# Weighted layer of a graph network: adjacency blocks in a ring of two, built between the products

## What is computed

```python
msgs = feat[src_idx] * affine[:, None]
agg = jax.ops.segment_sum(msgs, dst_idx, num_segments=feat.shape[0])
gcn_feat = jnp.concatenate([feat, agg], axis=-1)
out = gcn_feat @ mlp_w.T + mlp_b
```

## Time and profile before

| | us |
|---|---|
| median of 3 runs | 3364.9 (3363.34 to 3366.77) |
| the profiled execution's own time | 3366.92 |
| its span in the trace | 3365.2 |
| its mean granted TensorE clock | 0.922 of full speed |
| the list of steps of the third layer, first build to first product behind it | 1530.6 to 2197.0 |
| busy over the span: TensorE, GpSimd, VectorE, ScalarE | 2892.9, 2182.4, 1785.0, 1142.1 |

### The profile page before, as it was taken

The page is one execution under the profiler, slowest core; times in us unless marked ns, Lnnn a source line. Parts: engine busy times, 40 slices in busy tenths (PEclk is TensorE's granted clock), DMA queues, the critical chain, the costliest instruction groups (busy, mean ns, idle before and its releaser), DMA issues. The chain is left out here.

```text
span 3365.2 us, 61823 instructions
## 1 busy us (share of the span) xinstructions
PE 2892.9 (86%) x22719; PEld 2463.9 (73%) x22719; DVE 1785.0 (53%) x5589; ACT 1142.1 (34%) x1908; POOL 2182.4 (65%) x2179
## 2 busy tenths in 40 slices
PE   1699999999799989987999999967988887877885
PEld 0477777778688868866778777766988787777775
DVE  6899996233423334347766757556433333333334
ACT  2655554000200001014656656543522222222223
POOL 3465552777477666747777777317777777777772
PEclk9799999999899999998999999968988888888886
DMA  7355555888677777862222222123222222222222
GB/s 161 137 179 191 189 190 187 285 278 279 213 247 270 268 253 241 285 212 43 44 47 46 46 47 46 24 54 82 54 52 46 53 46 52 53 45 53 53 45 50
DMA packets 163977, 433.17 MB, mean 129 GB/s; under 512 B 63604, under 2 KB 105514, under 8 KB 143581
## 3 DMA queue, kind: packets, MB, share of 16 engines
q1 hardware_dynamic: 93998, 304.72, 25.6%
q0 software_dynamic: 69680, 124.50, 16.7%
HBM read 335.49 MB, written 93.53 MB: 127 GB/s over the span
## 5 line engine op out<-in xcount | busy, mean ns | idle before, releaser
L829 POOL DMA_INDIRECT work_all<-parts_dram,idx_all x768 | 809.6, 1054 | 357.6 <-issue 228.0
L1414 PE MATMUL ps<-arena 128*128 128x288 bf16 x7154 | 1023.5, 288 | 0.0
L2002 POOL DMA_INDIRECT arena<-table,idx_all x696 | 663.6, 953 | 325.0 <-issue 210.3
L1414 PEld LDWEIGHTS ps<-arena 128*128 128x128 bf16 x7154 | 711.8, 100 | 174.1
L2304 PE MATMUL ps<-M,arena 128*128 128x96 f32 x1664 | 424.9, 355 | 172.3 <-DVE arena L2187 169.3
L1561 POOL DMA_INDIRECT arena<-table,idx_all x400 | 405.6, 1014 | 121.9 <-issue 121.3
L2304 PEld LDWEIGHTS ps<-M,arena 128*128 128x128 f32 x1664 | 324.0, 242 | 192.4 <-issue 190.9
L1245 PE MATMUL ps<-arena,spare 128*128 128x245 bf16 x975 | 291.8, 305 | 30.5 <-ACT arena L882 18.5
L2306 PE MATMUL ps<-arena 128*128 128x96 bf16 x2496 | 291.2, 235 | 0.0
L1805 PE MATMUL ps<-work_all,gathot 128*128 128x245 f32 x1100 | 277.2, 390 | 14.1 <-DVE gathot L1655 12.0
L882 ACT ACTIVATE arena<-ps 128x980 bf16<-128x980 f32 x234 | 231.2, 990 | 166.5 <-PE ps L1245 166.5
(11 more groups left out here) (407 smaller groups left out, 4553.3 us busy)
## 6 DMA issues: line engine op xcount, KB each, us to landing
arena<-blocks_dram SPq DMA_DIRECT2D x117, 1568.0 KB
blocks_dram<-arena SPq DMA_DIRECT2D x39, 1568.0 KB, 6.5
arena<-table,idx_all POOLq DMA_INDIRECT x1096
parts_dram<-arena SPq DMA_DIRECT2D x28, 504.0 KB, 3.2
work_all<-parts_dram,idx_all POOLq DMA_INDIRECT x768
arena<-eaT_dram SPq DMA_DIRECT2D x10, 624.0 KB, 5.2
eaT_dram<-arena SPq DMA_DIRECT2D x48, 104.0 KB, 2.5
arena<-qtable SPq DMA_DIRECT2D x104, 45.0 KB
```

Of the source, the lines that this page charges most:

```text
L829: eng.indirect_dma_start(out=gat_rows[kk % 3][:, u, :], out_offset=None, in_=parts_dram[:, :], in_offset=bass.IndirectOffsetOnAxis(ap=idx_ ...
L1414: last = nc.tensor.matmul(apply_ps[n % 2], blk[m % 3][:, b, :], Hs[:, b, :], start=b == 0, stop=b == NB - 1)
L2002: eng.indirect_dma_start(out=rows[g % NROW][:, u, :], out_offset=None, in_=table[:, :], in_offset=bass.IndirectOffsetOnAxis(ap=idx_all[:, ...
```

## The change

`wadj` becomes a ring of two blocks of 125 targets, in the same room. The list of steps is written anew: TensorE builds block 0 and four tiles more (29 tiles), then in each block 49 products of 125 columns, with 21 tiles of the next block built between them, one after every second or third product, and behind the last product four tiles of the block after that (LEAD). There are 22 rounds of 49 products in place of 11. The copies to `wadj` are 13 a block, the last of one tile; three PSUM banks take builds and one, always the same, takes the products. The first product of a block waits for all copies of that block and for the addition of the block before. Groups, edge features and node units are spread over the list by a clock in which a build counts 2 and a product 1.

```diff
@@ -53,10 +53,10 @@
     WBLK, WFIRST = 22, 44
-    PAIRS, PB, PT = WBLK // 2, 2 * BW, 2 * VW
+    PB, WUNITS = 2 * BW, -(-VW // 2)
     NODEW, NTW, NWG = WBLK * BW, WBLK * VW, NG - WFIRST
     NVW = -(-NTW // NVT)
...
@@ -1483,34 +1483,60 @@
         ws_rel, ws_w, ok_col = small[:, 40:41], small[:, 48:49], small[:, 56:57]
         sum_ps = ps6[0:F, 0:P]
         er_banks = ps45
-        build_ps = [flat(t[:, 4 * i:4 * i + 4, :])[:, 0:2 * KW].rearrange("p (b d) -> p b d", d=2 * WN) for t in (ps01, ps23) for i in range(2)]
+        build_ps = [flat(t[:, 4 * i:4 * i + 4, :])[:, 0:2 * KW].rearrange("p (b d) -> p b d", d=2 * WN) for t, i in ((ps01, 0), (ps01, 1), (ps23, 0))]
         def dense_ps(m):
-            bank = ((m + 1) * (PT // 2) + 3) % 4
-            return flat((ps01, ps23)[bank // 2][0:F, bank % 2 * 4:bank % 2 * 4 + 4, :])[:, 0:PB]
-        STEPS = PT + NB
-        TOTAL = PAIRS * STEPS
-        GROUP_AT = {(2 * k + 1) * TOTAL // (2 * NWG): k for k in range(NWG)}
-        EDGE_AT = {(2 * e + 1) * TOTAL // (2 * NG): e for e in range(NG)}
-        SUM_AT = {s + 4: k for s, k in GROUP_AT.items()}
-        ADD_AT = {(m + 1) * STEPS: m for m in range(PAIRS - 1)}
-        NODE_AT = {8 + (TOTAL - 40) * i // NODE_UNITS: i for i in range(NODE_UNITS)}
-        NODE_LAG = 4
+            return flat(ps23[0:F, 4:8, :])[:, 0:BW]
+        def ring(m):
+            return m % 2 * BW
+        def unit_tiles(u):
+            m, j = divmod(u, WUNITS)
+            return range(m * VW + 2 * j, m * VW + min(2 * j + 2, VW))
+        LEAD = 4
+        STEPS = []
+        for m in range(-1, WBLK):
+            ready = LEAD + m * VW + VW if m >= 0 else 0
+            inside = [] if m < 0 else [ready + (b + 1) * (VW - LEAD) // NB for b in range(NB)]
+            done = ready
+            for b, upto in enumerate(inside):
+                STEPS.append((False, m, b))
+                STEPS += [(True, t, 0) for t in range(done, min(upto, NTW))]
+                done = upto
+            STEPS += [(True, t, 0) for t in range(done, min(LEAD + (m + 2) * VW, NTW))]
+        TOTAL = len(STEPS)
+        assert sum(is_build for is_build, _, _ in STEPS) == NTW and TOTAL == NTW + WBLK * NB
+        CLOCK = [0]
+        for is_build, _, _ in STEPS:
+            CLOCK.append(CLOCK[-1] + (2 if is_build else 1))
+        def spread(count, first, last):
+            at = [first + (last - first) * (2 * i + 1) / (2 * count) for i in range(count)]
+            return {next(s for s in range(TOTAL) if CLOCK[s + 1] > a): i for i, a in enumerate(at)}
+        BUILD_AT = {t: s for s, (is_build, t, _) in enumerate(STEPS) if is_build}
+        LAST_AT = {m: s for s, (is_build, m, b) in enumerate(STEPS) if not is_build and b == NB - 1}
+        EVAC_AT = {BUILD_AT[unit_tiles(u)[-1]]: u for u in range(WBLK * WUNITS)}
+        assert all(BUILD_AT[unit_tiles(u)[0]] > LAST_AT[u // WUNITS - 2] for u in range(2 * WUNITS, WBLK * WUNITS))
+        GROUP_AT = spread(NWG, 0, CLOCK[-1])
+        EDGE_AT = spread(NG, 0, CLOCK[-1])
+        SUM_AT = {s + 9: k for s, k in GROUP_AT.items()}
+        ADD_AT = {LAST_AT[m]: m for m in range(WBLK - 1)}
+        NODE_AT = spread(NODE_UNITS, 16, CLOCK[-1] - 64)
+        NODE_LAG = 8
...
-        def built_at(s):
-            m, j = divmod(s, STEPS)
-            return m * PT + j if j < PT else None
+        assert len(GROUP_AT) == NWG and len(EDGE_AT) == NG and TOTAL // NWG > 10
...
@@ -1595,12 +1621,13 @@
                         eng.wait_ge(nd_mm, ND0 + i - 1)
                     nc.scalar.activation(node_xT[i % 2][0:F, 0:wide], node_T_ps[:, 0:wide], ACT.Copy).then_inc(nd_xT, 1)
-                def evacuate(q):
-                    eng.wait_ge(built, BUILT0 + 2 * q + 2)
-                    m, j = divmod(q, PT // 2)
-                    if m and j == 0:
-                        eng.wait_ge(wapplied, m)
-                    nc.scalar.activation(wadj[:, :, 2 * j * WN:2 * (j + 1) * WN], build_ps[q % 4], ACT.Copy).then_inc(evac, 1)
+                def evacuate(u):
+                    tiles, m = unit_tiles(u), u // WUNITS
+                    eng.wait_ge(built, BUILT0 + tiles[-1] + 1)
+                    if m >= 2 and u % WUNITS == 0:
+                        eng.wait_ge(wapplied, m - 1)
+                    at, wide = ring(m) + tiles[0] % VW * WN, len(tiles) * WN
+                    nc.scalar.activation(wadj[:, :, at:at + wide], build_ps[u % 3][:, :, 0:wide], ACT.Copy).then_inc(evac, 1)
...
@@ -1614,9 +1641,8 @@
                     nc.scalar.activation(er_sq[0:F, :], er_out[0:F, :], ACT.Square, accum_out=erst[e % 2][:, 1:2]).then_inc(er_stat, 1)
                 for s in range(TOTAL):
-                    t = built_at(s)
-                    if t is not None and t % 2:
-                        evacuate(t // 2)
+                    if s in EVAC_AT:
+                        evacuate(EVAC_AT[s])
                     if s in NODE_AT:
                         turned_rows(NODE_AT[s])
                     if s in EDGE_AT:
@@ -1701,7 +1727,7 @@
                     eng.wait_ge(wapplied, m + 1)
                     if groups:
                         eng.wait_ge(acc_done, groups)
-                    nc.vector.tensor_tensor(aggT[:, m * PB:(m + 1) * PB], aggT[:, m * PB:(m + 1) * PB], dense_ps(m), ALU.add).then_inc(added, 1)
+                    nc.vector.tensor_tensor(aggT[:, m * BW:(m + 1) * BW], aggT[:, m * BW:(m + 1) * BW], dense_ps(m), ALU.add).then_inc(added, 1)
...
@@ -1715,28 +1741,29 @@
                 link.done()
                 stray_sums()
                 hots(0)
-                groups = 0
+                groups = dense = 0
                 for s in range(TOTAL):
-                    t = built_at(s)
+                    is_build, t, _ = STEPS[s]
                     if s in ADD_AT:
                         add_dense(ADD_AT[s], groups)
-                    if t is not None and t + WKEYS - 1 < NTW:
+                        dense += 1
+                    if is_build and t + WKEYS - 1 < NTW:
                         keys(t + WKEYS - 1)
                     if s - 2 * NODE_LAG in NODE_AT:
                         node_sums(NODE_AT[s - 2 * NODE_LAG])
                     if s in SUM_AT:
-                        into_nodes(SUM_AT[s], s // STEPS)
+                        into_nodes(SUM_AT[s], dense)
                         groups += 1
                     if s in GROUP_AT and GROUP_AT[s] + 1 < NWG:
                         hots(GROUP_AT[s] + 1)
                     if s in EDGE_AT and EDGE_AT[s]:
                         add_stats(EDGE_AT[s] - 1)
                 for k in range(groups, NWG):
...
@@ -1797,18 +1824,19 @@
                 def build_tile(t):
                     eng.wait_ge(keys_up, BUILT0 + t + 1)
-                    q = t // 2
-                    if t % 2 == 0 and q >= 4:
-                        eng.wait_ge(evac, EVAC0 + q - 3)
-                    if t % PT == 6 and t > PT:
-                        eng.wait_ge(added, t // PT)
-                    nc.tensor.matmul(build_ps[q % 4][:, :, (t % 2) * WN:(t % 2 + 1) * WN], wsrchot[t % WKEYS],
+                    m, j = divmod(t, VW)
+                    u = m * WUNITS + j // 2
+                    if j % 2 == 0 and u >= 3:
+                        eng.wait_ge(evac, EVAC0 + u - 2)
+                    nc.tensor.matmul(build_ps[u % 3][:, :, (j % 2) * WN:(j % 2 + 1) * WN], wsrchot[t % WKEYS],
                                      wkeyhot[t % WKEYS][:, 0:KW].rearrange("p (b d) -> p b d", d=WN), start=True, stop=True).then_inc(built, 1)
                 def apply(m, b):
                     if b == 0:
-                        eng.wait_ge(evac, EVAC0 + (m + 1) * PT // 2)
-                    last = nc.tensor.matmul(dense_ps(m), X[:, b, :], wadj[:, b, :], start=b == 0, stop=b == NB - 1)
+                        eng.wait_ge(evac, EVAC0 + (m + 1) * WUNITS)
+                        if m:
+                            eng.wait_ge(added, m)
+                    last = nc.tensor.matmul(dense_ps(m), X[:, b, :], wadj[:, b, ring(m):ring(m) + BW], start=b == 0, stop=b == NB - 1)
...
@@ -1835,11 +1863,11 @@
                 eng.wait_ge(k_link, 12)
                 stray_products()
                 for s in range(TOTAL):
-                    t = built_at(s)
-                    if t is not None:
-                        build_tile(t)
+                    is_build, i, b = STEPS[s]
+                    if is_build:
+                        build_tile(i)
                     else:
-                        apply(s // STEPS, s % STEPS - PT)
+                        apply(i, b)
...
```

More of the change, by code:

```diff
@@ L55, in build @@
     WBLK, WFIRST = 22, 44
-    PAIRS, PB, PT = WBLK // 2, 2 * BW, 2 * VW
+    PB, WUNITS = 2 * BW, -(-VW // 2)
     NODEW, NTW, NWG = WBLK * BW, WBLK * VW, NG - WFIRST
     NVW = -(-NTW // NVT)
-    assert WBLK % 2 == 0 and PB * 4 <= 1024 and 4 * NVT <= 512 and NVW == 5 and NODEW <= NODE0 and WFIRST <= GFIRST
```

(14 more changed lines are left out.)

## The result

The changed kernel takes 3318.7 us (median of 4 runs, 3317.7 to 3319.9) beside 3365.8 for the kernel before on the same chip: a ratio of 0.9858, interval 0.9841 to 0.9874, **47 us faster**. The forecast was 3323 with a range of 3308 to 3348 and a chance of 0.90 for faster.

A forecast was written before the change was run, and what follows sets the result against it. VectorE was taken to bound the building stretches, GpSimd to be a close second floor. List end 2153.8 against 2197.0 gave gain 43, taken as 42: 3366.9 to 3324.9, less 2.0 for the median, 3323 us; range 3308 to 3348.

The forecast's parts named there:

- the 59 us: Building stretches of the kernel before: 359.5 us, 59 more than TensorE needs, laid to VectorE's pace of making keys.
- VectorE's work hardly changes, 72%: Whole list: VectorE's 445.5 us of work stays, spread over some 620 us, so 72% busy.
- Products of 125 columns, 0.107 a record: Applying blocks: 2156 narrow product records at 0.107 us each, 230.7 us in place of 228.5.
- Start, 1.8 + 3: List start: 1.8 us lost to the half-rate clock, 3 us to the first 29 tiles going at VectorE's pace.
- Block starts, 7: Twenty-one block starts: first products wait for the last copy, 7 us in all, between 0 and 52.
- What I had costed at nothing: Between products: VectorE's additions, keys, 286 copies and three build banks were said to add no waits, 0 us.
- GpSimd sets the end: 2153.8 against TensorE's 2145.7: List end: GpSimd's last gathers hold it at 2153.8 us; TensorE alone would be there at 2145.7.
- my own formula: List end by GpSimd: last gather's end 2144.0, landing 2.5, group 59's products 1.3, last steps 5.0, addition and start 1.0.
- The announced waits for gathered rows: Near the list's end: TensorE's groups would stand waiting for gathered rows, taking what TensorE gained beyond GpSimd's 2153.8 us.
- Load-bound products: Rival, narrow products: weight loads set 0.165 us a record, list 740 us, 3439 us in all; chance 0.05.
- ScalarE taking over at the block starts: Rival, block starts: 1.7 us each, 36 instead of 7, gain 22, 3343 us; chance 0.18 shared with slower GpSimd.
- GpSimd slower when builds go on all the time: Rival, gathers: cadence 1.36 us, list end 2178, gain 19, 3346 us; chance 0.18 shared with late ScalarE.

The follow-up runs named there:

- run 2: Kernel before, key compare left out for all tiles behind the first seven: ratio 0.991, list of steps 634.8 us.
- run 3: Kernel before, each tile's key compare split into two of half the width: ratio 1.0118, building stretches 405.6 us where they took 359.5.
- run 4: Changed kernel, each tile's key compare split into two of half the width: ratio 0.9852 to the kernel before, list 622.5 us.
- run 6: Changed kernel with LEAD = 0, no tiles of the next block before a block's first product: ratio 0.9914 to the kernel before, list 643.2 us.
- run 5: Changed kernel with LEAD = 25, ring of two blocks kept but nothing built between products: 3340.4 us, ratio 0.9915 to the kernel before, list 644.7 us.
- run 9: Changed kernel, two of eight gathers left out in each group behind the first six: median 3318.0 us, ratio 0.9852 to the kernel before.
- run 7: Changed kernel, four of eight edge-feature products left out in 103 of 104 groups: 3316.1 us, ratio 0.9845 to the kernel before.
- run 1: Kernel before, each pair applied as two passes of 125-column products, nothing built between them: ratio 1.0002, list 666.2 us.
- the second profile: Changed kernel unedited, run and profiled once more: 3318.0 us, ratio 0.9852 to the kernel before, list 622.4 us.

## Why the prediction was right, point by point

- **VectorE was what the building half waited for.** Shown in both directions (runs 2 and 3), and that the change frees TensorE from it (run 4). But the 59 us have two causes, and the prediction laid nearly all of them to the first: run 2 leaves some 28 us standing while the waits for keys have nearly gone, and most of these stand for the last copy of each pair. The change covers this wait with the lead tiles (run 6) and the one for keys with the spreading (run 5). The sum priced the block starts by themselves, at 7 us, so it did not suffer.
- **VectorE's work hardly changes, 72%.** It reads 471.8 us, 76%, where 445.5 stood. The durations of its instructions, summed by line, rose only from 555.7 to 559.4 us, 1.7 of it for the additions. The rest of the 26 is overlap that is gone: busy time counts overlapping instructions once, and spread out they overlap by 88 us instead of 110.
- **Products of 125 columns, 0.107 a record.** Measured 0.106 in the change and 0.1075 by itself. The choice of row (same stationary form, cadence and not duration) was the one that mattered for the sign.
- **Start, 1.8 + 3.** The 29 tiles took 19.5 us with 58 build records, two groups and three edge groups, 16.1 us of work: 3.4 lost where 4.8 was priced, granted clock 0.90.
- **Block starts, 7.** 4.6 us on the load row, 2.5 of them the last start alone (2.1 on the product row), the one with a single tile before it:

```profile
2135.49 0.58 PE L1831 MATMUL ps<-work_all,gathot 128*128 128x245 f32 x2
2138.17 4.09 PE L1839 MATMUL ps<-arena,X 128*96 128x125 f32 x36 [2.10 <-ACT arena L1630]
```

  ScalarE's edge groups delayed few of the others. What I had costed at nothing, keys and copies in front of builds, took 4.4 (6.4 less the 2.0 among the first 29 tiles) and 2.1.
- **GpSimd sets the end: 2153.8 against TensorE's 2145.7.** This is the step that failed. The end came at 2151.7 and TensorE set it, 6 us later than its own sum said: 1.1 because the list began at 1531.7, the rest mainly the waits before builds just named and build records at 0.210 between products, where the sum has 0.207. GpSimd's last gather,

```profile
2136.28 0.95 POOL L1587 DMA_INDIRECT work_all<-table,idx_all  x1 [0.30 <-issue]
```

  ended at 2137.2, 6.8 us earlier than before. That is a cadence of (2137.2 - 1515.9) / 480 = 1.294 in place of 1.31, and rows landed after 1.7 us, not 2.5. With these two values my own formula gives 2137.2 + 1.7 + 1.3 + 5.0 + 1.0 = 2146.2, 5.5 us ahead of TensorE's end. The announced waits for gathered rows did not come in either profile, fewer gathers gained nothing (run 9), and the waits appeared only when TensorE was relieved by 22.7 us (run 7) or, for 1.9 us, when the gathers went slower (run 5). The two errors, 8 us too late for GpSimd and 6 too early for TensorE, met near the truth. That the forecast end is within 2.1 us of the measured one is luck; that it lies in the range is not, since the floor of either engine does.
- **The rivals.** Load-bound products: no (run 1). ScalarE taking over at the block starts: no, though without the lead tiles it would have been 23 us (run 6). GpSimd slower when builds go on all the time: it went slightly faster.
- **The size.** 42 us forecast; 47 in the medians, 46.5 in the list, 44.0 with the second profile. The sum had no term for the clock behind the start: some 3.5 us lost before the change, 0 and 1.7 in the two profiles after it.

## What to carry to other kernels

When one engine is full in one kind of stretch and idle in the next, and its ring holds only a few items, set the two kinds of work between each other. Here the whole change took 46.5 us off the list, about half of it by this order alone, where leaving out the key compare took off 31.6; and the price, twice as many fp32 products of half the width (125 columns), was nothing. Judge it by the starts of successive records and by the waits of the weight loads: busy sums and idle time of overlapping products hide most of the loss, and the load waits show somewhat more than it. A finer ring also multiplies its hand-over waits: give each a cover (a few builds ahead, the last copy a few products early), and look at the one hand-over for which the cover runs out.

## What the runs showed that I had not expected

- An added compare of half the width cost VectorE 0.097 us, although instructions of 80 columns follow each other at 0.245 us: widths do not tell this cost, the kind of instruction may (the short ones have two operations and two column operands, the compare one). That was not measured apart.
- The cadence of GpSimd's gathers went with the order of the other engines' work: 1.31 us in the kernel before, 1.294 in the changed one, and (2165.2 - 1515.4) / 480 = 1.354 with builds in bursts (run 5), where single gathers took up to 5.6 us (4.9 before, 4.0 in the changed kernel). These are single executions, and why it is so was not tried.
- The 1165 us behind the list, the same code in all runs, took between 1157.6 and 1173.3 us in the profiles. A few microseconds of a change are better read in its own stretch than in the total.
